# Expert-stage token repeats moved wholly to DMA, output sums moved from VectorE to ScalarE and GpSimd

## The reference, cut to what matters

```python
t = t + ffn(_ln_t(t), router_w, router_b, expert_w, expert_b)   # t: (8, 4096, 32)

def ffn(x, router_w, router_b, expert_w, expert_b):
    router_probs = softmax(x @ router_w + router_b, axis=-1)
    top_p, top_i = top_k(router_probs, 2)
    top_p = top_p / sum(top_p, axis=-1, keepdims=True)
    expert_out = einsum('bnd,edc->bnec', x, expert_w) + expert_b
    gathered = take_along_axis(expert_out, top_i[..., None], axis=2)
    return einsum('bnk,bnkc->bnc', top_p, gathered)
```

## Time and profile before

| | |
|---|---|
| median of 3 runs | 396.14 us |
| the profiled execution | 396.52 us, of which its span is 394.4 us |
| TensorE busy | 355.4 us (90%) |
| VectorE busy | 334.9 us (85%) |
| ScalarE busy | 260.4 us (66%) |
| GpSimd busy | 162.4 us (41%) |
| mean granted TensorE clock | 0.98 of full speed |

### The profile page before, as it was taken

One profiled execution on the slowest core, in us unless ns is written; L12 is line 12 of the kernel. 1 busy time (PEld: TensorE's weight loads), 2 busy tenths in 40 slices (PEclk: granted clock), 3 DMA queues, 4 the chain that ended last, 5 costly groups with the idle time before them and its releaser, 6 DMA issues.

```text
span 394.4 us, 12569 instructions
## 1 busy us (share of the span) xinstructions
PE 355.4 (90%) x5318; PEld 186.3 (47%) x5318; DVE 334.9 (85%) x435; ACT 260.4 (66%) x448; POOL 162.4 (41%) x191
## 2 busy tenths in 40 slices
PE   5998599999999999999999999898889897768894
PEld 2556366566666656566566556465321221111121
DVE  1598989898898889998998889999878999996785
ACT  3665787878878888768788887764663674324431
POOL 8610000220220220786551220687783468348543
PEclk9999999999999999999999999999998999896998
DMA  7700000220000000000002000033223444443541
GB/s 308 299 3 3 2 3 2 55 57 2 4 2 3 2 2 3 2 2 3 2 3 57 3 2 2 3 78 79 62 66 102 136 128 111 131 125 94 148 141 53
DMA packets 12870, 22.49 MB, mean 57 GB/s; under 512 B 2960, under 2 KB 5136, under 8 KB 12432
## 3 DMA queue, kind: packets, MB, share of 16 engines
q1 hardware_dynamic: 12240, 19.93, 17.4%
q10 hardware_dynamic: 576, 1.77, 1.1%
HBM read 5.96 MB, written 4.19 MB: 26 GB/s over the span
## 4 chain that ended last, share of the span: by engine, by line
PE 62%; DVE 23%; ACT 6%; issue 6%; POOL 2%; DMA 1%; POOLq 0%; DVEq 0%; ACTq 0%
PE psum L611 13%; PE psum L628 9%; PE psum L596 7%; PE psum L636 4%; PE psum L547 4%; PE psum L762 4%; PE psum L571 3%; DVE neg_max L1156 3%; PE psum L444 3%; DVE probs L1299 3%; PE psum L566 3%; DVE window_work L1159 3%; PE psum L580 2%; PE psum L774 2%; DVE probs L1296 2%
## 5 line engine op out<-in xcount | busy, mean ns | idle before, releaser
L327 POOL TENSOR_TENSOR o_norm<-o_tok,o_rden 128x128 f32<-128x128 f32 x64 | 25.4, 417 | 169.6 <-DVE o_rden L1169 169.6
L611 PE MATMUL psum<-weights_sb,window_work 128*128 128x128 f32 x512 | 81.6, 281 | 6.4 <-DVE window_work L1159 4.2
L896 ACT ACTIVATE probs<-psum 128x512 f32<-128x512 f32 x128 | 74.7, 594 | 17.5 <-PE psum L611 15.3
L1159 DVE TENSOR_TENSOR window_work<-psum,neg_max 128x1024 f32<-128x1024 f32 x64 | 78.4, 1225 | 2.2
L611 PEld LDWEIGHTS psum<-weights_sb,window_work 128*128 128x128 f32 x512 | 57.2, 140 | 48.7 <-issue 27.8
L1156 DVE TENSOR_REDUCE neg_max<-psum 128x16 f32<-128x1024 f32 x64 | 76.8, 1199 | 1.5 <-PE psum L596 1.5
L628 PE MATMUL psum<-probs,v_cols 128*32 128x64 f32 x2048 | 54.8, 225 | 0.4 <-DVE o_tok L1167 0.2
L628 PEld LDWEIGHTS psum<-probs,v_cols 128*32 128x32 f32 x2048 | 34.8, 109 | 28.2 <-issue 24.8
L880 ACT ACTIVATE stage<-k_sb,weights_sb 128x512 f32<-128x512 f32 x64 | 44.1, 719 | 0.0
L1167 DVE STREAM_TRANSPOSE o_tok<-psum 128x512 f32<-128x512 f32 x32 | 22.9, 716 | 20.4 <-PE psum L628 20.3
L596 PE MATMUL psum<-stage 32*64 32x256 f32 x1024 | 35.8, 387 | 2.7 <-DVE window_work L1159 2.0
(11 more groups left out here) (131 smaller groups left out, 607.0 us busy)
## 6 DMA issues: line engine op xcount, KB each, us to landing
stage<-act_all SPq DMA_DIRECT2D x144, 64.0 KB, 2.0
out<-out_sb SPq DMA_DIRECT2D x16, 256.0 KB, 2.0
stage<-in_x SPq DMA_DIRECT2D x3, 1024.0 KB, 11.9
gate_rows<-gate_parts SPq DMA_DIRECT2D x16, 128.0 KB, 2.6
weights_sb<-weights ACTq DMA_DIRECT2D x1, 811.5 KB, 15.1
stage<-in_x SPq DMA_DIRECT2D x1, 768.0 KB, 5.0
gate_f<-gate_sel ACTq DMA_DIRECT2D x1, 512.0 KB, 11.1
weights_sb<-weights ACTq DMA_DIRECT2D x1, 320.0 KB, 7.9
```

Source lines behind the costliest of these rows:

```text
L327: last = pool.tensor_tensor(o_norm[:, hf, :, p * 16:p * 16 + 16].rearrange("p g (b d) -> p g b d", b=2), t[:, p * 8:p * 8 + 8, :].rearrang ...
L611: last = nc.tensor.transpose(bank[TURN_BANKS[v % 2]][:, b * P:b * P + P], heads.rearrange("p h k -> p (h k)"), const["c_ident"][:, :])
L896: nc.scalar.activation(probs[:, w % 4, :], bank[TURN_BANKS[w % 2]][:, :], ACT.Exp).then_inc(exp_done, 1)
L1159: nc.vector.tensor_tensor(shifted_unit[:, unit % 2, :, :, :], t, m_t.unsqueeze(3).to_broadcast([P, IMG, HEADS, TOK]), ALU.add).then_inc(sh ...
```

## The change

- `x_rep` becomes three slots of **two chunks** each (two in `stage`, the third in columns of `x_win` that the gates of quads 0 and 1 use until they are done). A transfer now moves 32 rows of 1024 numbers (4 KB), twice as much as before.
- All images of all chunks are repeated by DMA: for the pairs of chunks 0 and 1 all 16 transfers by SyncE; from pair 2 on three images (12 transfers) by SyncE, and image 0 by ScalarE's queue, one transfer after each half's gate copy (`repeat_block`). `replicate` on TensorE, `keep_tokens` on ScalarE and the four copies that make `centre_rep` on VectorE are gone.
- The output sum leaves VectorE: ScalarE copies the bank to `y_sb` (`keep_sum`), GpSimd adds `act_all` (`combine`), both in half 1 of the next chunk. `y_sb` lies in `v_cols`. Only chunk 15 is still added by VectorE. `bias` waits for ScalarE's copy in place of the sum.
- Gate step 21 goes from VectorE to GpSimd (half 6), and step 22 on GpSimd from half 6, behind the product, to half 7, ahead of it.
- SyncE's queue is reordered: repeats of a pair are issued in even chunks, the gates of quad 1 and the repeats of pair 2 ahead of the first store, and the store of chunk c - 1 comes last in chunk c.
- TensorE's `side` has only the normalisation, with fewer waits.

```diff
@@ slots, waits, repeats @@
-SPLITS, SLOTS = 3, 4
+SPLITS, SLOTS = 3, 3
-        x_rep = stage[:, :].rearrange("p (s b n) -> p s b n", s=SLOTS, b=IMG)
+        x_reps = [t.rearrange("p (b u n) -> p b u n", b=IMG, u=2)
+                  for t in (stage[:, 0:half], stage[:, half:2 * half], x_win[:, 0:half])]
+        q_two = out_sb
+        y_sb = v_flat[:, 0:2 * CHUNK].rearrange("p (u n) -> p u n", u=2)
...
+        def repeat_pair(engine, pair, images, done, blocks=range(4)):
+            at = slice(pair * 2 * CHUNK, (pair + 1) * 2 * CHUNK)
+            for b in images:
+                for e in blocks:
+                    engine.dma_start(x_reps[pair % SLOTS][C * e:C * e + C, b, :, :],
+                                     act_all[C * b:C * b + C, at].rearrange("p (u n) -> p u n", u=2)
+                                     ).then_inc(done[pair % SLOTS], 16)
+        def wait_slot(engine, pair):
+            if pair >= SLOTS:
+                engine.wait_ge(y_step, (pair - SLOTS) * 4 + 4)
+            elif pair == 2:
+                engine.wait_ge(gate_step[1], GATE_OPS + ONE)
+            elif pair == 1:
+                engine.wait_ge(score_ps, CHUNKS * 2)
...
-            for h, n in ((1, 6), (4, 14), (6, 22), (7, 23), (8, 26), (8, 27), (9, 29)):
+            for h, n in ((1, 6), (4, 14), (6, 21), (7, 22), (7, 23), (8, 26), (8, 27), (9, 29)):
@@ SyncE @@
             for c in range(CHUNKS):
-                if c + 3 < CHUNKS:
-                    repeat_tokens(c + 3)
-                if c % QUAD == 2 and c // QUAD + 1 < QUADS:
+                if c == 1:
+                    move_gates(1)
+                    repeat_tokens(2)
+                if c >= 2 and c % 2 == 0 and c // 2 + 2 < CHUNKS // 2:
+                    repeat_tokens(c // 2 + 2)
+                if c % QUAD == 2 and 2 <= c // QUAD + 1 < QUADS:
                     move_gates(c // QUAD + 1)
-                sp.wait_ge(summed, c + 1)
-                sp.dma_start(out_v[:, c // BANDS, c % BANDS, :], out_sb[:, c % 2, :]).then_inc(stored[c % 2], 16)
+                if c >= 1:
+                    store(c - 1)
+            store(CHUNKS - 1)
@@ GpSimd @@
+            def combine(c):
+                pool.wait_ge(y_kept, c + 1)
+                wait_past(pool, stored[c % 2], c // 2 * 16)
+                pool.tensor_tensor(
+                    out_sb[:, c % 2, :].rearrange("p (y win x) -> p win y x", win=NW, y=WS),
+                    y_sb[:, c % 2, :].rearrange("p (win y x) -> p win y x", win=NW, y=WS),
+                    act_all[:, c * CHUNK:c * CHUNK + CHUNK].rearrange("p (win y x) -> p win y x", win=NW, y=WS),
+                    ALU.add).then_inc(summed, 1)
...
+                    if eh == 1 and c >= 1:
+                        combine(c - 1)
@@ TensorE @@
-                wait_past(pe, summed, c - 1)
+                wait_past(pe, y_kept, c - 1)
...
-                    replicate(ahead, 0)
@@ ScalarE @@
+            def repeat_block(h):
+                if h in (SLOTS + 1, SLOTS + 2):
+                    wait_slot(act, 2)
+                    first = 2 * (h - SLOTS - 1)
+                    repeat_pair(act, 2, range(1), reps_by_act, blocks=range(first, first + 2))
+                pair, e = (h + 7) // 4, (h + 7) % 4
+                if SLOTS <= pair < CHUNKS // 2:
+                    wait_slot(act, pair)
+                    repeat_pair(act, pair, range(1), reps_by_act, blocks=(e,))
+            def keep_sum(c):
+                act.wait_ge(y_step, c * 2 + 2)
+                wait_past(act, summed, c - 1)
+                nc.scalar.activation(y_sb[:, c % 2, :], bank[6 + c % 2][:, :], ACT.Copy).then_inc(y_kept, 1)
...
-                    if eh == 0 and c + REP_FIRST < CHUNKS:
-                        keep_tokens(c + REP_FIRST, 0)
+                    repeat_block(c * 2 + eh)
@@ VectorE @@
-            HALF_STEPS = ((0, 1, 2), (3, 4, 5), (7, 8), (9, 10, 11, 12), (13,), (15, 16), (17, 18, 19, 20, 21), (24,))
+            HALF_STEPS = ((0, 1, 2), (3, 4, 5), (7, 8), (9, 10, 11, 12), (13,), (15, 16), (17, 18, 19, 20), (24,))
...
-                    if eh == 0 and c >= 1:
-                        combine(c - 1)
```

More of the change, by code:

```diff
@@ L182, in metaformer_block @@
         reps_in = [sem(f"reps_in{k}") for k in range(SLOTS)]
-        rep_ps = sem("rep_ps")
-        rep_done = sem("rep_done")
+        reps_by_act = [sem(f"reps_by_act{k}") for k in range(SLOTS)]
         raw_done = sem("raw_done")
@@ L200, in metaformer_block, with x_rep, wait_tokens @@
         REP_FIRST = 2
[L202 to L216, removed]
+        def x_rep(c):
+            return x_reps[c // 2 % SLOTS][:, :, c % 2, :]
+        def wait_tokens(engine, c):
+            pair = c // 2
+            k, turns = pair % SLOTS, pair // SLOTS
+            engine.wait_ge(reps_in[k], 16 * ((16 if k < REP_FIRST else 12) + 12 * turns))
+            by_act = 4 * turns + (0 if k < REP_FIRST else 4)
+            if by_act > 0:
+                engine.wait_ge(reps_by_act[k], 16 * by_act)
+        def repeat_pair(engine, pair, images, done, blocks=range(4)):
[12 more added lines that the diff above has]
+                engine.wait_ge(score_ps, CHUNKS * 2)
         def wait_past(engine, s, n):
@@ L271, in move_gates, with repeat_tokens, store @@
                                  gate_parts[32 * j:32 * j + 32, :, :]).then_inc(gates_in[j], 16)
[L273 to L284, removed]
+            def repeat_tokens(pair):
+                sp.wait_ge(x2_done, min(pair * 2 + 2, CHUNKS) + X2)
+                wait_slot(sp, pair)
+                repeat_pair(sp, pair, range(0 if pair < REP_FIRST else 1, IMG), reps_in)
+            def store(c):
+                sp.wait_ge(summed, c + 1)
+                sp.dma_start(out_v[:, c // BANDS, c % BANDS, :], out_sb[:, c % 2, :]).then_inc(stored[c % 2], 16)
             repeat_tokens(0)
@@ L734, in _ @@
                 chunk(m, m % 2, final=(m == CHUNKS - 1))
-            def replicate(c, first_bank):
-                for b in range(2):
-                    rows = slice(32 * b, 32 * b + 32)
-                    last = nc.tensor.matmul(bank[first_bank + b][:, :], centre_rep[rows, :],
-                                            act_all[rows, c * CHUNK:c * CHUNK + CHUNK], start=True, stop=True)
-                last.then_inc(rep_ps, 1)
             def gate_pair(c, eh, pair):
@@ L818, in _ @@
                     gate_pair(c, eh, 1)
-                    side(c, eh)
                     if eh == 1:
+                        side(c)
                         experts(c, 0)
@@ L1030, in _ @@
                     copy_gates(c, eh)
+                    if eh == 1 and c >= 1:
+                        keep_sum(c - 1)
                     if c * 2 + eh in late_act:
@@ L1114, in regroups @@
                                       ).then_inc(regroup_ready, 1)
-                for b in range(IMG):
-                    rows = slice(C * b, C * b + C)
-                    nc.vector.tensor_copy(centre_rep[rows, :].rearrange("p (e c) -> p e c", e=IMG),
-                                          const["c_centre"][rows, rows].unsqueeze(1).to_broadcast([C, IMG, C]))
             constants()
```

51 lines of the change are left out of this document (16 added, 35 removed).

## The result

The kernel with the change takes 399.11 us (median of 19 runs, 397.40 to 401.51), the kernel before 396.14 (19 runs, 394.14 to 398.69). The ratio is 1.0064, with a 95% interval of 1.0045 to 1.0083. The forecast was 393.2 us and faster. The profiled execution took 397.73 us, 4.1 us over the 393.6 that the sum gave for it, with a span of 395.8. It is the third fastest of the 19, so the traces show only 1.2 us of the loss (397.73 against 396.52), where the ratio gives 2.5. Verdicts therefore go by the ratios, turned into time against 396.14 us.

A forecast was written before the change was run, and what follows sets the result against it. VectorE was taken to bound chunks 2 to 9. A lead of 4.0 us less 0.1 and 1.0 gave 2.9 off 396.52, so 393.6; the median lies 0.4 lower, hence 393.2 us, range 389.5 to 397.5.

The forecast's parts named there:

- the paragraph on the transfers: SyncE's queue: 128 KB lands after 2.0 us, twelve repeats issue in 7.4 us, first store in time; cost 0 to 1.5 us.
- Chunk 2: gain 2.6: VectorE in chunk 2: a 2.0 us wait and a 0.6 us sum go, a lead of 2.6 us at chunk 3.
- Quads: Chunks 2 to 9: GpSimd's list and ten waiting VectorE steps in turn, 31.0 us a quad against 31.4; lead 2.8 us.
- Run-out of the gates: From step 20 of quad 3 to experts(11,0): twelve GpSimd instructions take 14.65 us; loss 0.3, lead 2.5 us.
- The last chunks: experts(11,0) to experts(15,0): 18.15 us against 20.5, gain 2.3, gates about 0.8 us late for chunk 12; net +1.5, lead 4.0.
- The end: -0.1: After the last experts: GpSimd's sum of chunk 14 ends with the last product, VectorE still adds chunk 15; loss 0.1 us.
- Clock: -1.0: TensorE's clock: more half-clock spells after idle times, bounds 0 and 3 us, taken as a loss of 1.0 us.
- C: Rival: late first store or gates stop GpSimd, two stops of 1.5 us, 396.2 us, no change; chance 0.12.
- A: Rival: the VectorE-GpSimd port lock costs 0.75 us more on each of ten VectorE steps a quad, 399.2 us; chance 0.20.
- B: Rival: GpSimd keeps up and VectorE's list decides, a quad takes 28.5 us, 388.8 us; chance 0.14.

The follow-up runs named there:

- e6: e3 without ScalarE's repeats, so image 0 of chunks 4 to 15 is not repeated and outputs are not the reference's: 393.5 us, 0.9933 of the kernel before.
- e9: The changed kernel, two output places, with gates first and six repeats then a store in each chunk of SyncE's queue: 393.94 us, 0.9939 of the kernel before.
- e3: The changed kernel with four output places and the gates ahead of the repeats in SyncE's queue: 392.79 us, 0.9909 of the kernel before.
- e1: The changed kernel with four places for the output sum in place of two, queue unchanged: 396.63 us, 1.0012 of the kernel before.
- e2: The changed kernel with the gates of quads 2 and 3 ahead of the same chunk's repeats in SyncE's queue: 401.89 us, 1.0116 of the kernel before.
- e12: e3 with the output sums of chunks 8 to 14 on VectorE and those of chunks 0 to 7 on GpSimd: 392.59 us, 0.9904 of the kernel before.
- e10: e9's queue order with four places for the output sum: 391.69 us, 0.9897 of the kernel before.
- e11: e3 with gate step 21 back on VectorE and step 22 back behind GpSimd's product of half 6: 391.62 us, 0.9885 of the kernel before.
- e5: e3 with the output sums back on VectorE: 394.01 us, 0.9939 of the kernel before.
- e8: The kernel before with the output sums alone moved to ScalarE and GpSimd, its queue and TensorE's repeats unchanged: 416.18 us, 1.0508 of the kernel before.

## Why the prediction was wrong, step by step

**The step that failed** is the paragraph on the transfers: "64 KB repeats and 256 KB stores both land after 2.0 us, so 128 KB gets 2.0 too", then the issue time of 12 x 0.62 us, and "Cost 0, up to 1.5 if issues are slower". Both prices came from rows in which the DMA engines were under half busy (shares of 0.45 in the earlier trace rows). For the landing the page of the kernel before even had a transfer of that very size, the moves of gates, and it was not 2.0 us:

```profile
gate_rows<-gate_parts SPq DMA_DIRECT2D x16, 128.0 KB, 2.6
```

What was missing was the rate at which the engines are full, and a row of the kernel before had it. Two windows of the kernel before, the first one with its earliest repeats and little else on the DMA engines, the second the expert stage:

```profile
257.00:282.00 25.00, 22.35 (x423) 14.14 (x422) 23.55 (x31) 14.00 (x26) 18.25 (x23) 1.00 0.34 83
...
275.00:394.40 119.40, 98.02 (x612) 25.20 (x610) 99.25 (x136) 53.81 (x92) 66.96 (x57) 0.93 0.39 108
```

The expert stage of the changed kernel:

```profile
275.00:395.80 120.80, 88.07 (x556) 21.99 (x556) 90.54 (x119) 46.44 (x80) 89.18 (x74) 0.91 0.64 165
```

The first row says 83 / 0.34 = 244 GB/s when full, and the changed kernel has 241 at 1.01. Over the stage the change takes the share from 0.39 to 0.64, and since the repeats come in bursts, a burst meets full engines. From 294.49 to the first store the queues hold four moves of gates, twelve repeats of SyncE and seven of ScalarE, 23 DMAs of 128 KB or 3.0 MB. An estimate from these rows is 12.5 us at 241 GB/s, so until 307.0 to move them. The forecast had the store issued at 304.2; it was 307.82.

By the forecast's own prices both stores would have come in time: landed at 306.4 and, twelve issues and a landing later, at about 314. GpSimd was ready for its places at 308.16 and 316.18 (310.86 - 2.70 and 319.87 - 3.69). By the measured ones they landed near 310.8 and 319.8, which gives the two stops. e6 shows that the pace of the queue goes with the bytes, and e9 that the stops go with the order. The changed kernel with fewer bytes and two places was not run, so no run parts the loss between the two.

1. *Chunk 2: gain 2.6.* The sum and the 1.98 us wait did go. The lead at chunk 3 was 1.35, because the stage began 0.3 later and step 2 took 1.83 us for 0.75: it stood for a GpSimd instruction. In e3 the lead there is 2.65, as step 2 meets no such instruction. That is the exception: in e1, e2, e6 and e9 to e12 step 2 took 1.80 to 1.87 us, and chunk 2 took 8.6 us for 10.22 before, a gain of 1.6. So the term was too large by the 1.1 us that one such wait costs. e3 then gave its extra back: chunk 4 waited 1.57 us for its repeats.
2. *Quads.* The forecast says 31.0 us a quad and a lead of 2.6 kept through chunk 5; the two fit together only if 31.0 is the second quad and the first takes 29.2. Measured were 32.53 and 29.88. Without the stops e3 has 31.38 and 30.31, with two waits of VectorE in its first quad (1.57 us for repeats and 1.80 for TensorE). e10, e11 and e12 lack these and have 29.42 and 30.31, 29.29 and 29.00, 29.43 and 29.91:

```profile
294.45:323.87 29.42, 23.12 (x128) 5.63 (x120) 26.88 (x37) 16.41 (x29) 21.97 (x18) 0.94 0.86 222
323.87:354.18 30.31, 21.15 (x104) 4.44 (x104) 27.02 (x37) 9.52 (x16) 25.83 (x21) 0.80 0.86 230
```

So the first quad was sized rightly, and the second 0.7 to 2.0 us too long. The way to 31.0, GpSimd's list and ten steps of VectorE one after another, is not what bounded it. VectorE was busy 26.91 of the 29.88 us and waited for GpSimd once, for step 23, while GpSimd idled 4.0:

```profile
355.81 0.71 DVE L1251 STREAM_TRANSPOSE std_pair<-x_win 128x512 f32<-128x512 f32 x1 [1.95 <-POOL x_win L393]
```

VectorE's list (26.9) and GpSimd's sum (mean 1.34 us, most of them near 1.28) were right. GpSimd's busy time was 21.39 and 25.85, forecast 24.8. The prediction also puts the gain without the lock at some 6 us; from its own numbers it is 7.2 ((31.0 - 26.9) x 1.75).
3. *Run-out of the gates.* Step 20 of quad 3 ends at 352.1, experts(11,0) starts at 366.90: 14.8 us, forecast 14.65. Right.
4. *The last chunks.* Turns of 4.75 us in chunks 13 to 15 (376.88, 381.63, 386.38): right. From experts(11,0) to experts(15,0) the forecast had 18.15 us; e3 needs 384.37 - 366.39 = 17.98. After needed 22.31. Of these 4.2 us more, 2.78 are the wait for the gates of quad 3, where the forecast had 0.8. The repeats ahead of them began at 359.19, when chunk 9 was done as the forecast had it, and took 8.29 us, not 7.4. The remaining 1.4 are the late gates' consequence: chunk 12's products were not made beforehand, and experts(11,1) ran at the lower clock, 1.93 us for 1.06.
5. *The end: -0.1.* The last sum starts 1.13 us after the last experts begin before (390.12 and 391.25) and 1.18 after (391.42 and 392.60). Nothing to speak of, as forecast.
6. *Clock: -1.0.* The mean granted clock of the execution is 0.973, before 0.980. The spells at half clock after 327.27 and 370.74 stand right behind stops and are part of their cost. e3 has 0.965, lower still, and its span is 3.4 us shorter than before. What the clock takes by itself was not measured, so the term of 1.0 us is neither shown nor refuted.

**The rivals.** C was the right one: late stores and gates stop GpSimd, with the product and the steps behind its sum. Its price was two stops of 1.5 us. Measured were stops of 2.70 and 3.69 us on GpSimd, the second of which reached VectorE as 4.54, and one of 2.78 us on TensorE for the gates. It had a chance of 0.12 because "2.0 us landings at every size" was held against it, the same reading as above. A, the lock, gave a time near the measured one by another way: the twenty steps of VectorE with both inputs in SBUF took 13.15 us in the two quads before and 14.11 after, 0.05 a step and not 0.75, and e5 shows no gain from taking the sums off GpSimd. B, VectorE's list as what decides, describes the second quad better than the forecast does, but its 28.5 us was not reached in any run (29.00 in e11 at the least), and the stops hid it in the changed kernel.

e3's span of 391.0 against the forecast's 391.5 looks like a confirmation, but is partly luck: its lead at chunk 6 was 0.4 where 2.6 was forecast, and the last chunks gave back what was missing. e10, which gained 4.7, followed the forecast's leads more closely after chunk 3. What stands is the direction of the gains and their size to 1 or 2 us. The term that failed is the late stores and gates. It was set at 0 to 1.5 us for the stores and 0.8 for the gates; taking both away was worth 4.8 us of span, or 6.1 by the ratios.

## What to carry to other kernels

Before costing a change that moves more bytes, divide the rate by the DMA share in a window of the same kind of transfer: that is the ceiling, and landing and issue times read at half load don't hold near it. In a queue that waits in order, ask of each entry what stands behind it, and put small transfers that an engine waits for (stores that free a buffer, gates) between parts of a burst, not behind it. Test two suspected stops together as well as alone, since removing one can show nothing while the other stands.

## What the runs showed of the hardware

- Repeats between places of SBUF, 32 partitions a DMA, fill all 16 DMA engines at about 240 GB/s (1.01 at 241, 1.03 at 236), while the loads from HBM at the start reach more at a lower share, as the window from 10 to 20 us of the changed kernel shows (292 GB/s at 0.70, or 417 when full). By the Trainium skill (SBUF — State Buffer, "The DMA port swizzle") a transfer over 32 partitions uses half of the ports, with about 218 GB/s as its limit and twice that over 128. The trace agrees in kind only: from 301.5 to 307 us nothing but repeats is under way, and the rate is 231 GB/s at a share of 1.01, above the page's limit. Here the measurement decides.

```profile
10.00:20.00 10.00, 9.65 (x151) 5.33 (x149) 4.87 (x8) 6.97 (x15) 6.07 (x11) 1.00 0.70 292
...
301.50:307.00 5.50, 4.34 (x18) 1.19 (x10) 5.43 (x8) 2.09 (x5) 4.19 (x4) 1.00 1.01 231
```

- With full engines a DMA of 128 KB lands after 3.0 us and one of 256 KB after 2.8, against 2.0 for 64 and 256 KB, and SyncE's repeats take 0.65 to 0.82 us each to issue instead of 0.62.
- A store whose semaphore is not there yet holds all that stands behind it in SyncE's queue: moving the sums alone cost 5% (e8).
- Back-to-back GpSimd instructions did not shut VectorE out. Steps with two SBUF inputs waited 0.05 us more each on average, though single ones took 1.83 for 0.75. At times GpSimd was the one to stand: its sum at 348.01 took 1.74 us for 1.27, while VectorE's step 16 ran its usual 0.69 us from 347.92.
